# A graph network on one core: who makes the one-hots of the node tiles in the three convolutions, and when the sums are added

## The reference

```python
for i in range(3):
    mv = proj(mobius_matvec(W[i], h, c), c)
    h = proj(mobius_add(mv, hyp_bias, c), c)
    ht = logmap0(h, c)
    msgs = edge_weight[:, None] * ht[edge_col]              # fetch 200,000 rows of 64
    agg = segment_sum(msgs, edge_row, num_segments=6250)    # add them up by target node
    h = proj(expmap0(relu(logmap0(proj(expmap0(agg, c), c), c)), c), c)
```

## Time and profile before

| | |
|---|---|
| median of three executions | 14,566.06 us |
| profiled execution, its own time | 14,585.36 us |
| its span, first to last instruction | 14,583.5 us |
| mean granted TensorE clock | 0.673 of full speed |
| busy share of the span: PE, DVE, ACT, POOL | 65%, 70%, 28%, 73% |

### The profile page before, as it was taken

The page is one execution under the profiler, slowest core; times in us unless marked ns, Lnnn a source line. Parts: engine busy times, 40 slices in busy tenths (PEclk is TensorE's granted clock), DMA queues, the critical chain, the costliest instruction groups (busy, mean ns, idle before and its releaser), DMA issues.

```text
span 14583.5 us, 379790 instructions
## 1 busy us (share of the span) xinstructions
PE 9509.5 (65%) x89162; PEld 8547.0 (59%) x89163; DVE 10155.7 (70%) x46548; ACT 4114.1 (28%) x13780; POOL 10612.6 (73%) x10932
## 2 busy tenths in 40 slices
PE   0000006777778888788887888887555555788888
PEld 0000006777767777677776777777444444777777
DVE  7870007777776666666666888888766666888888
ACT  1000000000000000000000888887222222677777
POOL 3777777777767777677776777776677777677776
PEclk9995558888888888888888555555555555555555
DMA  2101112222211111111111111111111111111111
GB/s 100 27 25 26 26 26 48 41 42 41 38 27 26 27 27 27 27 27 27 27 27 26 28 28 27 27 27 23 28 26 26 27 27 26 28 27 27 27 27 29
DMA packets 499490, 443.36 MB, mean 30 GB/s; under 512 B 291533, under 2 KB 316749, under 8 KB 498254
## 3 DMA queue, kind: packets, MB, share of 16 engines
q0 software_dynamic: 349696, 337.89, 14.0%
q1 hardware_dynamic: 149454, 102.38, 2.5%
HBM read 368.39 MB, written 65.20 MB: 30 GB/s over the span
## 4 chain that ended last, share of the span: by engine, by line
PE 35%; issue 18%; DVE 17%; POOL 15%; DVEq 8%; DMA 6%; ACT 1%; POOLq 0%; ACTq 0%; SPq 0%
PE bank L1463 16%; PE bank L1438 11%; POOL packed L423 10%; POOL G L442 6%; DMA G<-table,idx 5%; DVEq L705 3%; PE bank L1520 3%; DVE OH L722 2%; PE bank L1532 2%; PE bank L1451 1%; PE bank L1509 1%; DVE OHB L733 1%; DVEq L707 1%; DVE OHT L761 1%; PE bank L1536 1%
## 5 line engine op out<-in xcount | busy, mean ns | idle before, releaser
L442 POOL DMA_INDIRECT G<-table,idx x9360 | 9084.3, 971 | 3264.8 <-issue 2412.9
L1463 PE MATMUL bank<-UZ,OHT 128*128 128x192 bf16 x15600 | 2086.4, 260 | 544.8 <-DVE OHT L761 544.8
L1438 PE MATMUL bank<-G,OH 128*128 128x64 f32 x9984 | 1686.3, 301 | 598.1 <-DVE OH L722 454.9
L423 POOL DMA_INDIRECT packed<-Y,slab_pos x1568 | 1528.1, 975 | 670.5 <-issue 494.7
L1356 ACT ACTIVATE OHB<-bank,const 128x512 bf16<-128x512 f32 x159 | 109.3, 688 | 6729.7 <-PE bank L1451 6729.7
L1463 PE MATMUL bank<-UZ,V 128*128 128x192 bf16 x14976 | 1992.8, 259 | 0.0
L1438 PEld LDWEIGHTS bank<-G,OH 128*128 128x128 f32 x9984 | 1496.1, 217 | 772.2 <-DVE OH L722 693.9
L1463 PEld LDWEIGHTS bank<-UZ,OHT 128*128 128x128 bf16 x15600 | 1505.8, 111 | 584.6 <-DVE OHT L761 563.1
L1438 PE MATMUL bank<-ZR,OH 128*128 128x65 f32 x6656 | 1765.6, 419 | 1.3 <-DVE ZR L829 1.3
L1438 PEld LDWEIGHTS bank<-ZR,OH 128*128 128x128 f32 x6656 | 1623.9, 334 | 1.9 <-DVE ZR L829 1.7
L722 DVE TENSOR_SCALAR OH<-const,DL,W 128x128 f32<-128x128 f32 x4992 | 1561.2, 368 | 0.2 <-issue 0.2
(11 more groups left out here) (281 smaller groups left out, 18632.0 us busy)
## 6 DMA issues: line engine op xcount, KB each, us to landing
G<-table,idx POOLq DMA_INDIRECT x9360, 2.5
packed<-Y SPq DMA_DIRECT2D x42, 640.0 KB, 17.4
UZ<-packed SPq DMA_DIRECT2D x104, 256.0 KB, 2.7
Y<-in_payload SPq DMA_DIRECT2D x98, 256.0 KB
packed<-Y,slab_pos POOLq DMA_INDIRECT x1568
table<-Y SPq DMA_DIRECT2D x6, 1690.0 KB, 5.5
idx<-SRC SPq DMA_DIRECT2D x624, 8.0 KB
X<-in_x SPq DMA_DIRECT2D x1, 1568.0 KB, 8.8
```

Of the source, the lines that this page charges most:

```text
L423: pool.indirect_dma_start(out=packed_rows, out_offset=bass.IndirectOffsetOnAxis(ap=slab_pos[:, h, c:c + 1], axis=0), in_=slab[:, h, c, :], ...
L442: pool.indirect_dma_start(out=G[:, 2 * q + c, :], out_offset=None, in_=table, in_offset=bass.IndirectOffsetOnAxis(ap=idx[:, h, j:j + 1], a ...
L1438: o = pe.matmul(ps_a[r % 2][:, 0:w], OH[:, q, c, :], parts[c], start=c == 0, stop=c == 1)
L1463: o = pe.matmul(ps_rows[c // 2][:, c % 2 * 3 * D:(c % 2 + 1) * 3 * D], tile_hot(tile)[:, c * P:(c + 1) * P], table_parts[:, tile, :, :].re ...
```

## The change

In the convolutions alone:

- One-hots: of the 49 tiles those with number 2, 5, 8, ..., 47 (16 tiles, `SHARE = 3`) are made by ACT in two instructions of 128x512, (tile - code) squared and then relu(1 - that), the second behind a wait for the first; DVE makes the other 33. ACT's loop `gcn_pass` now makes tiles and codes in turn.
- Slots: seven instead of eight, in `OHT`, `V`, `OHB` and `ZR`; `code` moves from `OHB` to `E8S`.
- Sums: four PSUM banks in turn instead of two, and DVE adds a group three steps later instead of one; PE's sums wait for the addition of four groups earlier.
- Row numbers: PE spreads them by four fp32 transposes instead of four products with the identity, at step 6 instead of 13, and DVE copies them at step 3 instead of 10.

The loops of PE, DVE and ACT's other passes keep their hints for the branch back (`steps`). The core of the diff:

```diff
-SLOTS = 8
+SLOTS = 7
+GCN_LAG = 3
+SHARE = 3
@@ slots and banks
-        code = OHB[...][:, 0:ON_CHIP * P]
+        code = E8S[...][:, 0:ON_CHIP * P]
+        slot_homes = [(OHT, 0), (OHT, P * BODY // 2), (V, 0), (V, P * BODY // 2), (OHB, 0), (OHB, P * BODY // 2), (ZR, 0)]
+        by_scalar = [t for t in range(T) if SHARE and t % SHARE == SHARE - 1]
+        by_vector = [t for t in range(T) if t not in by_scalar]
+        ps_sums = [bank[5], bank[6], bank[1], bank[0]]
+        sums_bank = [u % 4 for u in range(BODY)]
@@ DVE
                     for tile in range(u * TILES_A_STEP, min((u + 1) * TILES_A_STEP, T)):
+                        if tile in by_scalar:
+                            continue
                         need(v, tile_used, j + max(tile - SLOTS + 1, 0))
                         v.tensor_scalar(tile_hot(tile), code, float(tile), None, ALU.is_equal).then_inc(tile_ready, 1)
-                        v.tensor_tensor(acc, acc, ps_a[r % 2][:, 0:D], ALU.add).then_inc(acc_done, 1)
+                        v.tensor_tensor(acc, acc, ps_sums[sums_bank[r]][:, 0:D], ALU.add).then_inc(acc_done, 1)
-                lag = {GCN: 1, ATT: 8, MLP: 7}[kind]
+                lag = {GCN: GCN_LAG, ATT: 8, MLP: 7}[kind]
-                    if live(0) and u == 10:
+                    if live(0) and u == 3:
                         choose(i + 1)
@@ ACT
+                def tiles(i):
+                    if n_a:
+                        a.wait_ge(code_ready, i + (n * (ITER + 1) + 1))
+                    for k, tile in enumerate(by_scalar):
+                        need(a, tile_used, i * T + (n * ITER * T + max(tile - SLOTS + 1, 0)))
+                        a.activation(tile_hot(tile), code, ACT.Square, scale=-1.0, bias=bins[:, tile:tile + 1]).then_inc(squared, 1)
+                        a.wait_ge(squared, i * n_a + (n * ITER * n_a + k + 1))
+                        a.activation(tile_hot(tile), tile_hot(tile), ACT.Relu, scale=-1.0, bias=ones[:, 0:1]).then_inc(tile_made, 1)
@@ PE
-                need(pe, acc_done, g + (n * NG - 1))
+                need(pe, acc_done, g + (n * NG + 1 - behind))
-                        o = pe.matmul(ps_code[:, c * P:(c + 1) * P], chosen[:, c:c + 1].to_broadcast([P, P]), ident,
-                                      start=True, stop=True)
+                        o = pe.transpose(ps_code[c // 4][:, c % 4 * P:(c % 4 + 1) * P], chosen[:, c:c + 1].to_broadcast([P, P]), ident)
+                        if tile in by_scalar:
+                            pe.wait_ge(tile_made, ...)
+                        else:
+                            pe.wait_ge(tile_ready, ...)
-                        if u == 13:
+                        if u == 6:
                             spread(i + 1)
```

More of the change, by code:

```diff
@@ L237, in build @@
         ps_ty = [bank[6], bank[1]]
-        ps_code = bank[4]
-        ps_rows = [bank[2], bank[3], bank[7], bank[0]]
+        ps_code = [bank[4]]
+        ps_rows = [bank[2], bank[3]] + ([bank[0]] if ON_CHIP > 4 else [])
+        ps_sums = [bank[5], bank[6], bank[1], bank[0]]
+        sums_bank = [u % 4 for u in range(BODY)]
+        sums_behind = [next(k for k in range(1, BODY) if sums_bank[(u - k) % BODY] == b) for u, b in enumerate(sums_bank)]
         packed = nc.dram_tensor("packed", (P, NS, PAY), F32).ap()
@@ L1349, in mlp_pass, with gcn_pass, codes @@
                 steps(a, body, 1)
-            def codes(n):
-                def made(i):
+            def gcn_pass(n):
+                n_v, n_a = len(by_vector), len(by_scalar)
+                def codes(i):
                     a.wait_ge(code_spread, i + (n * (ITER + 1) + 1))
-                    need(a, tile_ready, i * T + n * ITER * T)
-                    a.activation(code, ps_code[:, 0:ON_CHIP * P], ACT.Identity, bias=own_row).then_inc(code_ready, 1)
-                made(0)
-                with a.Fori(1, ITER + 1) as i:
-                    made(i)
+                    need(a, tile_ready, i * n_v + n * ITER * n_v)
+                    need(a, tile_made, i * n_a + n * ITER * n_a)
+                    for h in range(0, ON_CHIP, 4):
+                        wide = min(ON_CHIP - h, 4) * P
+                        o = a.activation(code[:, h * P:h * P + wide], ps_code[h // 4][:, 0:wide], ACT.Identity, bias=own_row)
+                    o.then_inc(code_ready, 1)
+                def tiles(i):
[6 more added lines that the diff above has]
+                        a.activation(tile_hot(tile), tile_hot(tile), ACT.Relu, scale=-1.0, bias=ones[:, 0:1]).then_inc(tile_made, 1)
+                codes(0)
+                tiles(0)
+                codes(1)
+                with a.Fori(1, ITER) as i:
+                    tiles(i)
+                    codes(i + 1)
             a.wait_ge(s_const, 16)
@@ L1432, in node_product, with sums @@
                     products(i, i % 2)
-            def sums(g, q, r, n, parts, w):
-                need(pe, acc_done, g + (n * NG - 1))
+            def sums(g, q, to, behind, n, parts):
+                need(pe, acc_done, g + (n * NG + 1 - behind))
                 for c in range(2):
-                    o = pe.matmul(ps_a[r % 2][:, 0:w], OH[:, q, c, :], parts[c], start=c == 0, stop=c == 1)
+                    o = pe.matmul(to, OH[:, q, c, :], parts[c], start=c == 0, stop=c == 1)
                 o.then_inc(agg_ready, 1)
@@ L1481, in body @@
                             pe.wait_ge(taken[u - fetched(n)], i + (n * ITER + 1))
-                        sums(g, u % 8, u % 2, n, [G[:, 2 * u + c, 0:D] for c in range(2)], D)
+                        sums(g, u % 8, ps_sums[sums_bank[u]][:, 0:D], sums_behind[u], n, [G[:, 2 * u + c, 0:D] for c in range(2)])
                 steps(pe, body, 0)
@@ L1552, in step @@
                         pe.wait_ge(zr_ready, g + (kb - 6))
-                        sums(g - 7, (u - 7) % 8, r, n, [ZR[:, r, c, :] for c in range(2)], ROW)
+                        sums(g - 7, (u - 7) % 8, ps_a[r % 2][:, 0:ROW], 2, n, [ZR[:, r, c, :] for c in range(2)])
                 steps(pe, with_tiles(step), 7)
```

23 lines of the change are left out of this document (14 added, 9 removed).

## The result

The changed kernel takes 14,500.1 us (median of 5 runs, 14,487.42 to 14,509.0), the kernel before 14,566.06 (5 runs, 14,562.98 to 14,582.17): a ratio of 0.9956, 95% interval 0.9945 to 0.9966. That is 66 us faster, where 82 were forecast. The profiled execution took 14,487.42 us and was the fastest of its five, while that of before, 14,585.36, lies above all five of its own.

The account below looks back on a forecast made before the run. The prediction took POOL's unbroken DMA issue to bound the convolutions. Less DMA lengthening (-79 us) and shorter pass ends (-3) made -82, from 14,566.06 to 14,484 us at the runs' median; range 14,428 to 14,570.

Parts of the forecast that it names:

- What bounds the kernel: Convolutions: POOL issues DMAs without pause, 28 an iteration at 0.977 + 0.305 us, and PE waits for it.
- The naive reading: Convolutions: DVE bound PE after all, so 16 x 0.2 us leave each iteration; -500 us, 14,066; chance 0.02.
- PE or ACT as the bound: Convolutions: PE at low clock, or ACT pairs over 2.2 us, set the pace; +800 us; chance 0.05.
- The lever: Convolutions: unbroken runs of DVE's one-hots lengthen POOL's DMAs, 131.8 us in all; moving 16 tiles to ACT shortens runs.
- two fifths of 131.8 us stay: Convolutions: runs shrink from 1.40 to 1.13 us, so fewer DMAs lie wholly within one; -79 us.
- goes with all of DVE's time in one-hots: Convolutions: any overlap lengthens DMAs, one-hot time falls by 17%; -22 us, -25 with the ends, 14,541; chance 0.19.
- The rival on dense runs: DVE, each step with a tile: additions that never wait make runs denser, lengthening DMAs; +131 us, 14,697; chance 0.09.
- ACT: Convolutions: 16 pairs at 1.5 us and a code take 25 of 35.9 us an iteration, hidden by POOL; cost 0.
- Slots, banks, transposes, lag: 0: Convolutions: seven slots, four banks, later additions and spreading by transposes stay hidden behind POOL; cost 0.
- Ends of the passes, -3: After each convolution's last fetched rows: DVE reads registers while PE still sums, about 1 us three times; -3 us.
- The sum: Whole kernel: -79 us of lengthening and -3 us at the ends of passes make -82 us.

Follow-up runs that it names:

- e8: Kernel before with a twenty-ninth indirect DMA in each convolution iteration, into a tile nobody reads; 14,772.3 us, ratio 1.0143.
- e3: Kernel before with DVE's tile one-hots 4 columns wide instead of 512, the remaining columns cleared once a pass; 14,417.0 us, ratio 0.9897.
- e2: Changed kernel with additions one step later instead of three, a third of the tile one-hots still on ACT; 14,486.2 us, ratio 0.9943.
- e6: Changed kernel with all tile one-hots back on DVE and additions one step later; slots, banks and transposes kept; 14,538.3 us, ratio 0.9983.
- e9: Changed kernel with 20 of 49 tile one-hots on ACT instead of 16, and additions one step later; 14,672.3 us, ratio 1.0074.
- e1: Changed kernel with all 49 tile one-hots back on DVE, additions still three steps later; 14,730.6 us, ratio 1.0115.
- e4: Changed kernel with every second tile one-hot, 24 of 49, on ACT; 14,919.8 us, ratio 1.0242.
- e11: Changed kernel with 12 of 49 tile one-hots on ACT and additions one step later, second run, on a slower chip; 19,534.1 us, ratio 0.9909.

## Why the prediction was right, and which step was mis-sized

**What bounds the kernel.** Right. POOL's 0.305 us ahead of each DMA stayed, and e8 shows that one more DMA costs 1.28 us of the convolutions' time. The naive reading (-500 us) and PE or ACT as the bound (+800 us) didn't come.

**The lever.** Right. e3 took the tile one-hots away and with them 115 of 132 us of lengthening; e2 and e6 differ only in who makes a third of them, and by 74 us. The gain sits in the convolutions. Their three lengths fell by 77.5 us, made up of 63.6 us of lengthening, 13.1 us of the execution's shorter median DMA (3 ns x 4,368), and 0.8 us of rest.

**The size, "two fifths of 131.8 us stay".** This term was mis-sized: 68.2 us stay, 52%. It gave 63.6 us and not 79, a miss of 15 us that the scatter of the measure could make by itself. The criterion behind it, a DMA that lies wholly within an unbroken run, comes near in the sums. With a lag of one a third on ACT leaves 67 of 141 us (48%), where the rule has 40%; two fifths leave 37 (26%), where it has 0.6 x 4 x 0.20 + 0.59 = 1.07 us and (1.07 - 0.95) / 0.45 = 27%. But the count doesn't bear it out. By the rule fewer DMAs lie within a run, and each costs what it did. From e6 to e2 and e9 their number fell only from 1,868 to 1,135 and 1,080 (61 and 58%), what each costs fell too, from 0.069 us to 0.029 and 0.019, and half of what is left lies on other DMAs. In the kernels where DVE makes all the one-hots and waits for PE, the criterion picks out the DMAs that are lengthened (121 of 132 us); in the others it doesn't, and least in e1. That the sums came near is partly luck. With narrow one-hots 17 of 132 stay (13%), and the rule has none, 0.59 being shorter than a DMA; 8 of the 17 are the five DMAs at the heads. Some of the rest in the changed kernel is the first convolution. By its own row 1,403.70 - 1,456 x 0.944 = 29.2 us stay there, and in the later two only 18.4 and 20.6; its DVE has 5,252 operations and not 4,370.

**The rival "goes with all of DVE's time in one-hots".** Out. It had 83% staying; 52% did. The Trainium skill, "SBUF — State Buffer", section "SBUF: two separate sides", has the lock that would give this rival if taken literally. The trace agrees that VectorE can hold GpSimd up (e1, 0.50 us in one DMA), and disagrees with any price per overlap: e3's weighted one-hots run beside the DMAs all through, and all that is left is 17 us in 4,368 of them. No run tells, though, which of DVE's instructions work in a two-port mode, so the disagreement is with the rival and not surely with the rule. Nor does a price per overlap with the tile one-hots alone fit: their time falls by a third, 67% should stay with a third on ACT and 60% with two fifths, and 48% and 26% do.

**The rival on dense runs.** Its loss is real, and it didn't come in this kernel. e1 has it: 172 us more lengthening than e6, and 615 more DMAs lengthened by 0.2 us or more than before, 3.9 an iteration. Its mechanism, more DMAs within unbroken runs, is not what the count shows. The argument against it (DVE has 23 us of work in 35.9 and must pause at the slots) was wrong: e1's DVE has 1,259 us of work in 1,897 and pauses at the slots too, and that doesn't help. What kept the changed kernel from it is ACT's share, the one thing in which e1 differs. The two halves of the change are not independent, and the forecast priced them one at a time.

**ACT.** Forecast 1.5 us a pair, measured 0.714 + 0.722 + 0.03 = 1.47; forecast 65% busy, measured 65%. In sequence a pair takes 1.37 us. The forecast's limit, 2.2 us for each of 16 pairs, leaves out ACT's waits for slots: with 24 pairs (e4) it is these that bring ACT's loop over POOL's.

**Slots, banks, transposes, lag: 0.** Right in the convolutions (e6 against before, e2 against after).

**Ends of the passes, -3.** The mechanism is right: DVE reads its registers beside PE's last sums. It gave 0.5 us at the first end and 1.1 at the second; the third, with a pause of 2.61 us whose cause stays open, is 0.3 us longer: -1.2 in all. In e1, which has the same lag and no such pause, the ends take 4.53, 4.54 and 4.27 us, and in e6, with a lag of one, 5.79, 5.74 and 5.78: there the lag gives 4.0.

**The sum.** -64 in place of -79 and -1 in place of -3 make -65; the medians show -66. That these agree so well is luck: e6 has the convolutions of before and is 25 us faster all the same.

**A better version.** None of the complete kernels is clearly faster than the changed one. e2 has 0.9943 (0.993 to 0.9957) against 0.9956 (0.9945 to 0.9966), and the intervals overlap.

## What to carry to other kernels

Look for the engine that issues at an even spacing, and not for the one with the largest busy share: here it was at 73%, and its spacing, 1.25 us from one DMA to the next, set the time. Where a neighbour lengthens its instructions, count over all of them before you trust a criterion read from one or two, and test an edit that takes a wait out of the neighbour together with the one that lightens its work: the wait was worth 172 us here as long as DVE made all the tile one-hots. Count what is moved to an idle engine against the bound engine's iteration, its waits for others included: 16 pairs were free, 20 no longer in the first convolution, and 24 nowhere.

## What the runs showed beside that

- A pass of which no line was changed took between 2,106 us (e6) and 2,222 us (e9), the attention pass; before and after have 2,129 and 2,127. In e9 it goes with DVE's wait "issue" at the head of the loop, 2.7 us and not 0.75. In so long a program a difference of 20 us between two kernels needs to be placed before it is explained.
- On two chips the same kernel before took 19,709 us and not 14,566, with the same granted clock over the span as elsewhere (0.67 in e11, 0.673 in before). e11's trace has pauses of about 2 us on POOL, which it puts down to PE or to "remote". The ratio between two kernels wasn't the same there either.
- A square and a dependent relu of 128x512 on ACT, the second in place, cost 1.47 us together, with 0.03 us between them, and 1.37 us each where such pairs follow one another; the lower bound from the 128x256 row was 1.02.
- In every kernel the DMAs at the heads of the convolutions are the longest in them: the second one of the later two passes takes 3.4 us and not 0.95.
